# One core, a two-layer attention and feed-forward program: the first output taken ahead of the second normalisation, a preparation piece behind it, and the fourth weighing put behind the next projection

## What is computed

```
x = x + wkv(w, u, layernorm(x), ctx)          # a recurrence over 256 steps
x = x + ffn(layernorm(x))                     # 256x256 matmul on values rounded to 8 bits
x = x + attention(layernorm(x), ctx)          # 16 query heads, 8 key heads; self and context
x = x + linear_attention(layernorm(x))        # along the batch, 16 small heads
```

## Time and profile before

| what | value |
|---|---|
| median of 3 runs | 826.28 us (825.75 to 826.7) |
| profiled execution | 826.89 us, span of the instructions 825.1 us |
| mean granted TensorE clock | 0.93 of full speed |
| TensorE busy | 662.8 us (80% of the span) |
| VectorE busy | 569.9 us (69%) |
| ScalarE busy | 422.2 us (51%) |
| GpSimd busy | 278.4 us (34%) |

### The profile page before, as it was taken

How to read it: one execution, slowest core, us unless ns; L and a number is a source line. 1 busy time by engine, 2 the same in 40 slices (tenths; PEclk the granted TensorE clock), 3 DMA queues, 4 the chain that set the end, 5 groups by cost and what they waited for, 6 DMA issues and landing times.

```text
span 825.1 us, 12899 instructions
## 1 busy us (share of the span) xinstructions
PE 662.8 (80%) x4279; PEld 514.7 (62%) x4279; DVE 569.9 (69%) x1358; ACT 422.2 (51%) x1370; POOL 278.4 (34%) x357
## 2 busy tenths in 40 slices
PE   3046877877888988999898989998998999968454
PEld 2035656654766776776677867776777777735333
DVE  4874566566748774888787667787763666666996
ACT  3125656555556654565655455656654566624221
POOL 5203353232312444343234533332331333323250
PEclk9566999899899999999999999999999999979768
DMA  7042434334143412233232322322222332200001
GB/s 237 0 154 90 157 99 167 131 114 144 35 172 105 113 73 89 90 120 131 96 104 90 90 75 105 91 90 92 99 92 79 101 101 79 78 1 1 0 1 51
DMA packets 32347, 77.03 MB, mean 93 GB/s; under 512 B 2814, under 2 KB 28058, under 8 KB 28186
## 3 DMA queue, kind: packets, MB, share of 16 engines
q1 hardware_dynamic: 32096, 76.20, 27.7%
q10 hardware_dynamic: 186, 0.02, 0.0%
HBM read 62.56 MB, written 13.65 MB: 92 GB/s over the span
## 4 chain that ended last, share of the span: by engine, by line
PE 51%; DVE 22%; issue 7%; ACT 7%; POOL 4%; DVEq 0%; ACTq 0%; POOLq 0%
PE bank L587 12%; PE bank L479 11%; PE bank L575 7%; PE bank L487 6%; PE bank L545 3%; DVE Cb L1497 3%; POOL rs L1109 3%; PE bank L611 3%; PE bank L669 2%; DVE WQ L1444 2%; PE bank L576 2%; ACT WQ L838 1%; DVE Qn L1465 1%; PE bank L601 1%; ACT square L873 1%
## 5 line engine op out<-in xcount | busy, mean ns | idle before, releaser
L587 PE MATMUL bank<-V,Pt 128*128 128x129 f32 x1024 | 144.4, 285 | 28.7 <-DVE Cb L1497 27.0
L587 PEld LDWEIGHTS bank<-V,Pt 128*128 128x128 f32 x1024 | 128.6, 195 | 61.1 <-DVE Cb L1497 50.0
L873 ACT ACTIVATE square<-bank 128x128 bf16<-128x128 f32 x384 | 101.3, 276 | 100.7 <-PE bank L479 60.3
L479 PE MATMUL bank<-WQ,xq 128*128 128x256 f32 (+1 forms) x1024 | 138.3, 288 | 4.1 <-DVE xq L1384 3.3
L479 PEld LDWEIGHTS bank<-WQ,xq 128*128 128x128 f32 x1024 | 129.0, 195 | 18.0 <-DVE nm L1483 9.0
L575 PE MATMUL bank<-QT,KTt 128*128 128x512 f32 x256 | 136.2, 614 | 2.4 <-POOL diag L1123 2.4
L1483 DVE TENSOR_REDUCE nm<-bank 128x2 f32<-128x512 f32 x128 | 82.1, 683 | 42.8 <-PE bank L562 42.7
L856 ACT ACTIVATE Pt<-bank 128x512 f32<-128x512 f32 x128 | 76.6, 598 | 64.5 <-PE bank L576 61.0
L1109 POOL TENSOR_TENSOR rs<-ve,mhalf 128x6 f32<-128x6 f32 x64 | 94.6, 1478 | 5.3
L1123 POOL TENSOR_TENSOR diag<-identb,nm 128x512 bf16<-128x512 bf16 x64 | 67.0, 1047 | 60.4 <-DVE nm L1483 60.4
L1116 POOL CAST KTh<-KTt 128x256 bf16<-128x256 f32 x32 | 12.7, 396 | 205.4 <-ACT KTt L883 205.4
(11 more groups left out here) (198 smaller groups left out, 1057.9 us busy)
## 6 DMA issues: line engine op xcount, KB each, us to landing
WQ<-wq_split SPq DMA_DIRECT2D x24, 1536.0 KB, 6.5
wq_split<-WQ SPq DMA_DIRECT2D x8, 1536.0 KB, 5.3
ism<-smooth_inverse SPq DMA_DIRECT2D x32, 256.0 KB, 4.6
wpst<-in_L_xattn_wproj SPq DMA_DIRECT2D x16, 256.0 KB, 4.9
wst<-in_L_xattn_wq SPq DMA_DIRECT2D x8, 256.0 KB, 3.0
wst<-in_L_xattn_wqx SPq DMA_DIRECT2D x8, 256.0 KB, 3.3
wst<-in_L_xattn_w_kv_x SPq DMA_DIRECT2D x16, 128.0 KB, 3.8
xs<-in_x SPq DMA_DIRECT2D x4, 256.0 KB, 5.6
```

What stands on the lines that cost most here:

```text
L479: last = nc.tensor.matmul(o[:, o0:o0 + n], xq[b % 2][:, p, k, ts], WQ[u % 2][:, part, k, w0:w0 + n], start=m == 0, stop=m == 2 * KT - 1)
L587: last = nc.tensor.matmul(OB[:, h * (P + 2):h * (P + 2) + P + 1], Pt[:, x, k, h * S + t * P:h * S + (t + 1) * P], V[u % 2][:, x, k, 0:P + ...
L873: last = A(square[:, t, h], head(t, h), ACT.Square, accum_out=ss[:, t, h:h + 1])
```

## The change

Three things are moved; no instruction is added, taken out or changed.

- On VectorE `outputs(u,0,0)` goes ahead of `normalise(u+1,1)` and of the second `low_weights`; `early` goes from ahead of them to behind the second `low_weights`, in every step but 4, where it stays ahead (at the wrap it now follows `normalise(u+1,0)`).
- On VectorE `end` goes ahead of `outputs(u,1,1)`.
- On TensorE `weigh(u,1,1)` goes behind `project(u+2,0)`.

```
@@ TensorE @@
                 weights(u + 2, (4,))
                 guard(u + 1, 0)
                 weights(u + 2, (5,))
-                weigh(u, 1, 1)
                 if (u + 2) % G and u + 2 < UNITS:
                     project(u + 2, 0)
+                weigh(u, 1, 1)
                 if step == 0:
                     turn_h(nb)
@@ VectorE @@
                 if u:
                     quantise(u - 1)
-                if nb:
-                    early(nb, step)
                 if (u + 1) % G == 0:
                     normalise(u + 1, 0)
+                if step == 4:
+                    early(nb, step)
                 low_weights(u + 2, (0,))
+                outputs(u, 0, 0)
                 normalise(u + 1, 1)
                 low_weights(u + 2, (1,))
-                outputs(u, 0, 0)
+                if nb and step != 4:
+                    early(nb, step)
                 low_weights(u + 2, (2,))
                 outputs(u, 0, 1)
...
                 maxima(u + 1, 0, 0)
                 maxima(u + 1, 0, 1)
-                outputs(u, 1, 1)
                 if nb:
                     end(nb, step)
+                outputs(u, 1, 1)
```

## The result

The changed kernel takes 846.98 us (843.64 to 847.84, 4 runs) against 826.01 (824.16 to 826.7) for the kernel before: ratio 1.025, 95% interval 1.0217 to 1.0283. It is slower, as forecast, but by 21 us where 8.8 were forecast, and outside the range of 829 to 843. The profiled execution took 843.64 us, with a span of 841.8; it is the fastest of the four, so the profile shows some 3 us less than the median. The two profiles differ by 841.8 - 825.1 = 16.7 us, so 4 of the 21 us stand in no profile.

The account below looks back on a forecast made before the run. It took TensorE, busy for 80% of the span, as the bound, then its waits for VectorE's outputs (24.6 us). Terms 2.2 - 3.2 - 6.8 = -7.8, and 1 for the clock, made 8.8 slower: 835.0 us, range 829 to 843.

Parts of the forecast that it names:

- clock term: TensorE's granted clock falling to 1.2 GHz at longer waits: bounds 0 and +6 us, +1 taken.
- the one case in unit 16: A wait of 2.13 followed by slow matmuls at 1.2 GHz, costing about 1.7 us more.
- Units 23 to 30: Last passes, most without an early piece: waits at second and fourth weighing go, small new ones come; gain 2.2 us.
- Step 2: Passes with four moved scans (turn of outputs, units 9 and 17): second output later; loss 2.5 us each.
- step 3: Passes with 2.2 of early work: third weighing 1.1 late, maximum delayed by 0.6; gain 0.3 us.
- Step 1: Passes with an early piece of 4.0: second output 0.6 later, exponentials delayed; loss 0.55 us at each of two units.
- Steps 6 and 7: Passes with early pieces of about 2.1 and 3.4: gains of 0.35 and 0.1 us.
- Weights' passes: Units 0 to 5: first output delays the second low weights, which free XB, and the turn of outputs; loss 6.8 us.
- Unit 0: First weights' pass: moved early piece ends near 100.2, third low weights start 2.1 late; loss 2.1 us.
- The first, a covered early piece: Rival: second output not waited for at the third weighing, early piece hidden; 818 to 820 us, chance 0.11.
- The second, weights' passes without loss: Rival: later turn of outputs caught up by ScalarE's and GpSimd's slack; 828 us, range 826.5 to 831, chance 0.18.
- The third, the clock falling in most of the new waits: Rival: TensorE's clock falls in most of the new waits; 840 us, up to 845, chance 0.13.

Follow-up runs that it names:

- filled: The changed kernel plus matmuls whose result nobody reads, put into TensorE's long waits; 831.75 us, ratio 1.0054 to the kernel before.
- weigh_only: The kernel before with only the fourth weighing moved behind the next projection and the end piece ahead of the fourth output; 815.92 us, ratio 0.9853.
- early_ahead: The changed kernel with the early pieces back at their old place ahead of first output and second normalisation; 824.06 us, ratio 0.9955 to the kernel before.
- low_first: The changed kernel, but in passes 0 to 5 the first output stands behind the second low weights, as before; 828.23 us, ratio 1.002 to the kernel before.
- old_weights: The changed kernel, but in passes of units 0 to 5 VectorE keeps the old order; 829.34 us, ratio 0.9997 to the kernel before.

## Why the prediction was wrong

**The step that failed is the clock term.** "Bounds 0 and +6 us; I take +1". It measures 4.6 to 7.5 by the estimates above, near or over its upper bound, and with the clock held up (`filled`) the changed kernel takes 831.75 us, inside the forecast range. The prediction weighed each long wait by the one case in unit 16, as if such a fall were an exception. The trace of the kernel before says otherwise: of its six waits over 2 us in units 0 to 22, five came with a stretch at 1.2 GHz (units 1, 2, 4, 5 and 16; not unit 8). Of the 13 such waits in new places in the changed kernel, 11 did (not units 6 and 9), and the passes went from 24 us at 1.2 GHz to 58. Units 1, 2 and 5, named as relieved, each have such a stretch after, since they got a new wait of 2.8 to 3.0 at the turn of outputs. Units 0, 14 and 22, where the clock falls too, were not named. The Trainium skill, "TensorE: Matmul & The Clock Gate", What's actually happening, says that the throttled state is the default and that activity releases it. Its rule was put down as the upper bound when it should have been the forecast; `filled`, in which activity in the waits kept the clock up, agrees with it.

**Waits: 7.8 forecast, 10.3 to 13 measured.** This is the second term that was too small. The mechanism held at most places, and the sign was wrong in steps 6 and 7 and in unit 23.
- *Units 23 to 30*: 2.2 gained forecast, 3.2 measured. Unit 25 lost 0.1 and not 0.45, unit 23 gained 0.6 where 0.15 was to be lost. What the sum left out there is that the power ends sooner: `weigh_only` alone shortens unit 23 by 0.6.
- *Step 2*: 2.5 forecast, 2.0 and 2.5 measured; *step 3*: gain 0.3 forecast, 0.6 measured; *step 5*: 0.15 and 0.13; *step 0*: nothing forecast, a gain of 0.5 measured; *step 4*: gain 0.5 forecast, 0.4 measured.
- *Step 1*: a loss of 0.55 forecast, 2.5 and 2.2 measured. Most of this is the clock; with it up in unit 8 and nearly so in unit 16 (`filled`) the two are at +1.1 and +0.8, a little more than forecast.
- *Steps 6 and 7*: gains of 0.35 and 0.1 forecast, losses of 0.3 and of 0.5 to 1.4 measured. In step 7 the loss is 0.5 with the clock up (`filled`), the rest is clock. With the early piece ahead (`early_ahead`) the two steps gain 0.8 and 1.1, so the moved early piece is the cause. That it holds up ScalarE and `halves` behind the third weighing is likely, but was not tried by itself.
- *Weights' passes*: 6.8 forecast, 11.6 measured. The chain through XB holds: the turn of outputs comes 3.92 behind its weighing in units 2 to 5, where it came 174.12 - 172.03 = 2.09 behind it in unit 3 before, so 1.83 later and 1.75 forecast. Unit 3 lost 1.8 where 2.05 was forecast, with one stretch of 3 us at the lower clock, and 1.5 with the clock up (`filled`). Unit 4 lost 3.2 where 1.9 was, with 10 us at the lower clock against 7 before.
- *Unit 0*: 2.1 forecast, 5.6 measured, 4.1 with the clock up. The early piece was priced by its old place, where its maximum took 0.88. In the new place it is

```profile
97.85 1.26 DVE L1264 TENSOR_TENSOR_SCAN tmp<-vec,tmp 128x256 f32<-128x256 f32 x2
99.21 2.70 DVE L1272 SCALAR_TENSOR_TENSOR tmp<-tmp,vec 128x256 f32<-128x256 f32 x2
101.83 1.11 DVE L1444 SCALAR_TENSOR_TENSOR WQ<-bank,vec,WQ 128x128 fp32r<-128x128 f32 x4
```

The maximum takes 2.70, as in unit 8, because GpSimd's subtraction now starts with it (99.19); at the old place GpSimd first waited for ScalarE's squares, and the subtraction came at 92.51, behind the maximum. The third low weights start at 101.83, not at 100.2. The rule of the Trainium skill, "SBUF — State Buffer", SBUF: two separate sides, was applied in the prediction to unit 8 and not to unit 0, where the move changed what the piece meets. The trace agrees with the rule there too.

**The rivals.** The first, a covered early piece, would have needed E below 1.1 us; `early_ahead` shows what it would have brought, 16 us in units 6 to 22, near the 13 worked out; 7.2 of them come from the moved weighing. The second, weights' passes without loss, is refuted by the 11.6 us that these passes lost; `low_first` shows the chain that makes most of it. The third, the clock falling in most of the new waits, is what happened, and the time lies above even its top of 845: priced too low, and added to waits that were too low as well.

**What stays open.** Why the gain of the moved weighing in units 1 to 5 differs between kernels (4.2 in `weigh_only`, 2.5 in `old_weights`); the two differ in where the clock fell (7 us in unit 5 of `old_weights`, none there in `weigh_only`), and no run separates this. Also open is why some waits of 2 us and more leave the clock up and others do not: 3.57 us at the turn of outputs in unit 17 came with a stretch at 1.2 GHz, the same 3.57 in unit 9 did not.

## What to carry to other kernels

An output that frees a bank can go ahead of other work on its engine only if nothing else in the queue is waited for sooner; here that held from unit 6 on (8.8 us won in units 6 to 22) and not where the second low weights freed a shared bank (19.5 us lost in units 0 to 5, both by `early_ahead` against `weigh_only`). Move a long piece to where the next consumer is furthest away, and give it its price at the new place, with what the neighbour engine then does. Where a move makes TensorE wait for some 2 to 4 us, count the slower matmuls after it as well as the wait, and look in the trace that you have for how often the clock fell at such waits. Try the parts of a change one by one, since here one part alone was worth 1.5%, the other cost 2.8%, and both together cost 2.5%, more than the sum.

## What the runs showed of the hardware

Matmuls that nobody reads, put into 13 waits of 2 to 4 us, kept the granted clock at 2.4 GHz for nearly all of the passes (3 us at 1.2 GHz instead of 58) and shortened them by 11.9 us, with the distances from weighing to turn unchanged. A microsecond at 1.2 GHz cost some 0.22 us here, and 0.35 between runs of the kernel before. One VectorE instruction pair, the maximum of step 1, took 0.88, 1.72, 2.70 or 2.71 us: 0.88 with GpSimd idle, 1.72 where GpSimd's subtraction began 0.4 behind it, 2.7 where both began together. And an instruction order that takes no wait away on paper, the projection ahead of a weighing, gained in part by letting a chain over two engines (squares, power) end 0.9 us earlier against TensorE.
